# Short products with activations standing, and an accumulation by transfer into the residual tile, in a fused expert and state-space kernel on one Trainium2 core

## The reference

```python
x = x + 0.5 * ffn(layernorm(x), w_router, w_gating, w_gate, w_up, w_down)
x = x + attn(layernorm(x), W_in, conv_w, ..., W_out)      # a Mamba block
x = x + 0.5 * ffn(layernorm(x), w_router, ...)            # the same weights again

def ffn(x, ...):                       # E = 8 experts, F = 512; dense, every expert for every token
    cw = softmax(x @ w_router) * softmax(x @ w_gating / 0.1)
    cw = cw / (sum(cw) + 1e-9)         # 8 weights per token
    h[e] = silu(x @ w_gate[e]) * (x @ w_up[e])
    return sum_e (h[e] @ w_down[e]) * cw[:, e]

def attn(x, ...):                      # d_inner 256, 16 states, conv of 4, dt_rank 64
    xs, z = split(x @ W_in)            # 2 x 256
    xc = silu(causal_conv(xs) + conv_b)
    dt, B, C = from xc @ W_x           # dt = softplus(... @ W_dt + b_dt)
    h_t = exp(dt_t * A) * h_{t-1} + dt_t * xc_t * B_t     # per feature and state
    y = sum_n h[:, n] * C[n] + xc * D_param
    return (y * silu(z)) @ W_out
```

## Time and profile before

| | |
|---|---|
| time, median of 3 runs | 1301.04 us (1297.74 to 1301.64) |
| the profiled execution's own time | 1303.95 us |
| its span in the profile | 1302.2 us |
| PE busy | 1259.6 us, 97% |
| DVE busy | 1121.7 us, 86% |
| ACT busy | 925.3 us, 71% |
| POOL busy | 366.8 us, 28% |
| moved by DMA | 208.55 MB, mean 160 GB/s |

### The profile page before, as it was taken

The page is one execution under the profiler, slowest core; times in us unless marked ns, Lnnn a source line. Parts: engine busy times, 40 slices in busy tenths (PEclk is TensorE's granted clock), DMA queues, the critical chain, the costliest instruction groups (busy, mean ns, idle before and its releaser), DMA issues.

```text
span 1302.2 us, 15232 instructions
## 1 busy us (share of the span) xinstructions
PE 1259.6 (97%) x4608; PEld 841.3 (65%) x4608; DVE 1121.7 (86%) x1468; ACT 925.3 (71%) x1757; POOL 366.8 (28%) x438
## 2 busy tenths in 40 slices
PE   5999799999999999999999999999999999999998
PEld 4666566666666666666666666666666665666665
DVE  3554599999999999999989999999999998998343
ACT  6545688878797878887948878698866887653421
POOL 0100134324232322433323332342323323332000
PEclk9999899999999999999999999999999999999899
DMA  6521488789788988987888978987888786895221
GB/s 204 134 54 33 100 177 197 160 176 196 161 181 184 181 173 188 208 177 169 183 180 188 194 171 178 181 191 170 188 175 186 174 186 149 186 197 119 50 64 41
DMA packets 125809, 208.55 MB, mean 160 GB/s; under 512 B 15008, under 2 KB 27808, under 8 KB 125728
## 3 DMA queue, kind: packets, MB, share of 16 engines
q0 software_dynamic: 52128, 94.92, 40.8%
q1 hardware_dynamic: 73600, 112.68, 32.8%
HBM read 109.77 MB, written 2.88 MB: 87 GB/s over the span
## 4 chain that ended last, share of the span: by engine, by line
PE 65%; DMA 12%; ACT 9%; DVE 8%; issue 5%; POOL 2%; SPq 0%; DVEq 0%; ACTq 0%; POOLq 0%
PE PS L734 23%; PE PS L679 13%; PE PS L681 13%; PE PS L680 13%; DMA Y<-HS 7%; DMA ACC<-YE 3%; DVE HS L943 2%; DVE HB L851 2%; DVE HS L951 2%; ACT DA L1090 1%; ACT HB L1024 1%; DMA BCB<-BCD 1%; ACT L1024 1%; PE PS L755 1%; ACT L1090 1%
## 5 line engine op out<-in xcount | busy, mean ns | idle before, releaser
L734 PE MATMUL PS<-HB,WD 128*128 128x512 f32 x1024 | 525.3, 594 | 0.0
L1024 ACT ACTIVATE HB<-PS 128x512 f32<-128x512 f32 x512 | 293.1, 596 | 279.8 <-PE PS L681 277.4
L851 DVE TENSOR_TENSOR HB<-PS,HB 128x512 f32<-128x512 f32 x512 | 347.2, 679 | 113.9 <-PE PS L681 71.7
L679 PE MATMUL PS<-XH,WG 128*128 128x512 f32 x512 | 386.6, 755 | 6.1 <-DVE XH L906 2.0
L1139 POOL DMA_DIRECT2D Y<-HS x252 | 219.7, 949 | 511.0 <-DVE HS L951 319.5
L734 PEld LDWEIGHTS PS<-HB,WD 128*128 128x128 f32 x1024 | 191.8, 189 | 44.3 <-issue 3.4
L679 PE MATMUL PS<-XH,WU 128*128 128x512 f32 x512 | 209.5, 409 | 10.1 <-DVE HB L851 9.8
L1127 POOL DMA_DIRECT2D ACC<-YE x110 | 104.1, 947 | 369.3 <-DVE YE L841 339.4
L681 PE MATMUL PS<-XH,WG 128*128 128x512 f32 x512 | 203.2, 397 | 0.0
L681 PE MATMUL PS<-XH,WU 128*128 128x512 f32 x512 | 202.0, 395 | 0.0
L680 PE MATMUL PS<-XH,WU 128*128 128x512 f32 x512 | 201.0, 393 | 0.0
(11 more groups left out here) (104 smaller groups left out, 1127.3 us busy)
## 6 DMA issues: line engine op xcount, KB each, us to landing
BCB<-BCD SPq DMA_DIRECT2D x128, 512.0 KB, 5.6
Y<-HS POOLq DMA_DIRECT2D x252, 256.0 KB, 6.7
CWB<-CWD SPq DMA_DIRECT2D x128, 256.0 KB, 4.3
ACC<-YE POOLq DMA_DIRECT2D x110, 256.0 KB, 5.3
XT<-in_L_attn_x_dram SPq DMA_DIRECT2D x8, 256.0 KB, 5.9
WD<-in_L_ffn_w_down_dram SPq DMA_DIRECT2D x8, 256.0 KB, 6.1
out_dram<-XT SPq DMA_DIRECT2D x8, 256.0 KB, 3.1
HS<-in_L_ffn_w_gate_dram SPq DMA_DIRECT2D x6, 256.0 KB, 5.0
```

What stands on the lines that cost most here:

```text
L679: pe.matmul(o, w[0], m[0], start=first, stop=False)
L734: pe.matmul(expert(g), WD[:, e, c, :], HB[:, i % NH, :], start=c == 0, stop=c == FC - 1).then_inc(S["m_dn"], 1)
L851: v.tensor_tensor(H, up(i), H, ALU.mult).then_inc(S["v_h"], 1)
L1024: a.activation(HB[:, i % NH, :], gate(i), ACT.Silu).then_inc(S["a_sil"], 1)
```

## The change

- `down` has HB standing and WD moving: for each block of 128 tokens, one f32 product of 128 columns, so four in place of one of 512. The expert's bank then has tokens on partitions and output features along the row, like XT.
- The weights of a position stay per token row, in CW (two buffers). `p_ct`, `cwt`, CWD, its stores, CWB and `cw_load` go. `acc` multiplies the bank by CW[:, :, e] broadcast along the features, always into YE.
- The transfer adds YE straight into XT. Expert 0 is added in this way too. In the first and the last position the last expert is added on DVE by four scalar_tensor_tensor of 128x128 that multiply, add and write XT. ACC, `acc_t` and `acc_add` go; x1 is ready when the last add has landed, and ACT and SP wait for that.
- `s_out` has Y standing and WO moving: four blocks of tokens times two halves, eight f32 products of 128 columns. The copy to XN and `s_tr` go; `s_add` reads the bank of `s_out`.
- In `timetable()` the costs follow (`down` 0.9 for 0.86, `s_out` 1.78 for 1.75, the last step of a position 5.5 for 5.0, at the ends 0.9 for 1.25), and LEAD is 2.0 for 2.4.

```diff
-LEAD = 2.4
+LEAD = 2.0
...
     def weigh(g):
         if g % E < E - 1 or g // E not in ENDS:
-            at = step("acc", g, after=clock["pe"] + SIGNAL["pe"], v=.61, p=.9) + (5.0 if g % E == E - 1 else 0.0)
-        else:
-            at = step("acc", g, after=clock["pe"] + SIGNAL["pe"], v=1.25)
-        weights["used"] = g + 1
-        weight_loads()
-        return at
+            return step("acc", g, after=clock["pe"] + SIGNAL["pe"], v=.61, p=.9) + (5.5 if g % E == E - 1 else 0.0)
+        return step("acc", g, after=clock["pe"] + SIGNAL["pe"], v=.9)
 
     def tail(p):
         kind, t = ORDER[p]
         at = weigh(p * E + E - 1)
-        acc_done.add(p)
-        yield from until(at + 1.0)
-        bk = yield from take()
-        at = step("acc_t", p, bk, pe=.6)
-        yield from until_v(at)
-        at = step("acc_add", p, bk[0], after=at, v=.61)
-        give(bk[0], "v_x1", p + 1, at)
         if kind == 0:
             x1[t] = at
+        else:
+            yield from until(at)
+            step("out", t)
...
         yield from until(at)
-        yield from rows_of_x()
         bk = yield from take()
-        at = step("s_out", t, bk, xn["by"], after=at, pe=1.75, a=.52)
-        give(bk[0], "a_wo", t + 1, at)
+        at = step("s_out", t, bk, after=at, pe=1.78)
         put.add(t)
-        yield from until(at)
-        bk = yield from take()
-        at = step("s_tr", t, bk, pe=.6)
-        xn.update(by=("m_to", t + 1), lock=False)
...
                     wt.wait_ge(S["v_h"], i + 1)
-                    pe.matmul(expert(g), WD[:, e, c, :], HB[:, i % NH, :], start=c == 0, stop=c == FC - 1).then_inc(S["m_dn"], 1)
+                    for j in range(SUB):
+                        z = pe.matmul(expert(g)[:, j, :], HB[:, i % NH, j * P:(j + 1) * P], WD[:, e, c, :],
+                                      start=c == 0 and j == 0, stop=c == FC - 1 and j == SUB - 1)
+                    z.then_inc(S["m_dn"], 1)
...
-                    for j in range(2):
-                        z = pe.matmul(bank(b), WO[:, j, :], Y[:, t % 2, j, :], start=j == 0, stop=j == 1)
+                    for j in range(SUB):
+                        for c in range(2):
+                            z = pe.matmul(bank(b)[:, j * P:(j + 1) * P], Y[:, t % 2, c, j * P:(j + 1) * P], WO[:, c, :],
+                                          start=c == 0, stop=c == 1)
...
                     wt.wait_ge(S["m_dn"], FC * (g + 1))
-                    wt.wait_ge(S[f"c_cwb{g % CR}"], 16 * (g // CR + 1))
-                    if e == 0:
-                        if p:
-                            wt.wait_ge(S["m_tz"], p)
-                        y = ACC[:, :]
+                    wt.wait_ge(S["v_cw"], p + 1)
+                    if e == E - 1 and p in ENDS:
+                        wt.wait_ge(S["c_acc"], 16 * added(p, E - 1))
+                        for j in range(SUB):
+                            X = XT[:, ORDER[p][1] % XR, j, :]
+                            z = v.scalar_tensor_tensor(out=X, in0=expert(g)[:, j, :], scalar=CW[:, p % 2, j, e:e + 1], in1=X,
+                                                       op0=ALU.mult, op1=ALU.add)
+                        z.then_inc(S["v_ye"], 1)
                     else:
-                        n = p * (E - 1) + e - 1
+                        n = added(p, e)
                         if n >= 2:
-                            wait_summed(wt, n - 2)
-                        y = YE[:, n % 2, :]
-                    v.tensor_tensor(y, expert(g), CWB[:, g % CR, :], ALU.mult).then_inc(S["v_ye"], 1)
-                    if e == E - 1 and p in ENDS:
-                        wt.wait_ge(S["v_ye"], g + 1)
-                        wt.wait_ge(S["c_acc"], 16 * added(p, E - 2))
-                        v.tensor_tensor(ACC[:, :], ACC[:, :], y, ALU.add).then_inc(S["v_acc"], 1)
+                            wt.wait_ge(S["c_acc"], 16 * (n - 1))
+                        v.tensor_tensor(YE[:, n % 2, :, :], expert(g), CW[:, p % 2, :, e].unsqueeze(2).broadcast_to([P, SUB, P]),
+                                        ALU.mult).then_inc(S["v_ye"], 1)
...
-                        gp.dma_start(ACC[:, :], YE[:, n % 2, :], accum_op=ALU.add).then_inc(S["c_acc"], 16)
+                    gp.dma_start(XT[:, ORDER[p][1] % XR, :, :], YE[:, n % 2, :, :], accum_op=ALU.add).then_inc(S["c_acc"], 16)
```

More of the change, by code:

```diff
@@ L29 @@
 NB = 4 - NG
-CR = 3
 HR = 4
@@ L403, in timetable @@
         if i >= LAG:
-            step("down", i - LAG, after=h_at[i - LAG], pe=.86)
+            step("down", i - LAG, after=h_at[i - LAG], pe=.9)
             nd += 1
@@ L435, in timetable @@
     for i in range(nd, total):
-        step("down", i, pe=.86)
+        step("down", i, pe=.9)
     run(tail(NPOS - 1))
@@ L480, in macaron_program @@
         XH = sb("XH", [P, 2, 2, T], F32R)
-        CWB = sb("CWB", [P, CR, T])
-        YE = sb("YE", [P, 2, T])
-        ACC = sb("ACC", [P, T])
+        YE = sb("YE", [P, 2, SUB, P])
         HB = sb("HB", [P, NH, T])
@@ L515, in macaron_program @@
         S = {}
[L516 to L519, removed]
+        for n in ("c_small c_con c_acc c_y0 c_y1 c_bcd o_x init w_hi w_lo dv "
+                  "m_g m_u m_dn m_tr m_lg m_win m_wx m_wt m_wo "
+                  "a_sil a_sum a_mean a_sq a_xn a_car a_xf a_xh a_exp a_neg a_rmh a_win a_tap a_yc a_dbl a_abs a_relu a_sexp a_soft a_yd a_da "
+                  "v_h v_sub v_norm v_cw v_ye v_mset v_rm v_halo v_cv v_bc v_db v_sc v_hc v_yz v_x2 v_dt v_dx v_y v_xl "
                   "p_ve p_rs p_nm").split():
             S[n] = ctx.enter_context(nc.semaphore(n))
-        for b in range(CR):
-            S[f"c_cwb{b}"] = ctx.enter_context(nc.semaphore(f"c_cwb{b}"))
         for b in range(BR):
@@ L551, in expert @@
         def expert(g):
-            return PS[:, NG + 2 + g % 2, :]
+            return PS[:, NG + 2 + g % 2, :].rearrange("p (j d) -> p j d", j=SUB)
         def added(p, n):
-            return p * (E - 1) - (p > 0) + n
+            return p * E - (p > 0) + n
         def wait_position(eng, p):
             if p in ENDS:
-                eng.wait_ge(S["v_acc"], 1 + (p > 0))
+                eng.wait_ge(S["v_ye"], (p + 1) * E)
             else:
[L564 to L572, removed]
+                eng.wait_ge(S["c_acc"], 16 * added(p, E))
         def carried(m):
@@ L663, in _ @@
                     sy.dma_start(XT[:, t % XR, :, :], xf[t]).then_inc(S[f"c_x{t}"], 16)
-                elif s[0] == "acc_add" and ORDER[s[1]][0] == 1:
-                    t = ORDER[s[1]][1]
-                    wt.wait_ge(S["v_x1"], s[1] + 1)
+                elif s[0] == "out":
+                    t = s[1]
+                    wait_position(wt, POSITION[1, t])
                     if nout:
@@ L764, in _ @@
                 elif k == "s_out":
-                    _, t, (b, at), by = s
+                    _, t, (b, at) = s
                     wait_count(wt, at)
                     wt.wait_ge(S["v_yz"], t + 1)
-                    for j in range(2):
-                        z = pe.matmul(bank(b), WO[:, j, :], Y[:, t % 2, j, :], start=j == 0, stop=j == 1)
+                    for j in range(SUB):
+                        for c in range(2):
+                            z = pe.matmul(bank(b)[:, j * P:(j + 1) * P], Y[:, t % 2, c, j * P:(j + 1) * P], WO[:, c, :],
+                                          start=c == 0, stop=c == 1)
                     z.then_inc(S["m_wo"], 1)
[L771 to L777, removed]
         @block.vector
@@ L818, in _ @@
                     wt.wait_ge(S["dv"], dv)
[L819 to L823, removed]
-                    if p:
-                        wt.wait_ge(S["c_cwd"], 16 * SUB * p)
-                    v.transpose(cwt[:, :], pq[:, :, :].rearrange("p j e -> p (j e)")).then_inc(S["v_cw"], 1)
+                    v.scalar_tensor_tensor(out=CW[:, p % 2, :, :], in0=lg[:, :, 2, :], scalar=0.5,
+                                               in1=sm[:, :].unsqueeze(2).broadcast_to([P, SUB, E]), op0=ALU.mult, op1=ALU.mult).then_inc(S["v_cw"], 1)
                 elif k == "acc":
@@ L851, in _ @@
                     v.tensor_tensor(H, up(i), H, ALU.mult).then_inc(S["v_h"], 1)
-                elif k == "acc_add":
-                    _, p, b = s
-                    X = XT[:, ORDER[p][1] % XR, :, :].rearrange("p j d -> p (j d)")
-                    wt.wait_ge(S["m_tz"], p + 1)
-                    v.tensor_tensor(X, X, bank(b), ALU.add).then_inc(S["v_x1"], 1)
                 elif k == "w_split":
```

60 lines of the change are left out of this document (11 added, 49 removed).

## The result

The changed kernel takes 1281.13 us (median of 4 runs, 1280.6 to 1281.49) against 1301.34 us before: ratio 0.9835, 95% interval 0.982 to 0.985, or 20.2 us less. The forecast was 1291, 10 us less. The direction was right and the size was not: the gain is twice the one that was summed.

The account below looks back on a forecast made before the run. PE, 97% busy, was taken as nearly full with DVE close behind; +22 +0.6 -3.5 -7.0 -24.8 +5 -1.7 = -9.4 us against the profiled execution, carried to the runs' median as 1291 us, range 1277 to 1313.

Parts of the forecast that it names:

- The products down: Each `down` on PE: eight load-paced pairs of 0.112 us, 0.90 us against 0.857, +22 us over 512 slots.
- The first rival: Eight pairs of each `down`: weight loads don't hide fully, 1316 at 0.118 a pair, 1353 at full 0.015; chance 0.18.
- the ratio that the prediction worked out from the Trainium skill: Each `down`: four short products cost 2.5 times one long one, 2.12 us, kernel up by about 645 us.
- SP's queue: CWB loads and CWD stores hold places ahead of BCB loads; removing them saves PE 9.1 us, and 1.3 at 185 to 191.
- The state stage's output: `s_out` as 16 pairs +0.6 us; `s_tr` gone -3.5 us of PE, plus its waits of 5.4 us.
- The end: Last multiply, add, transposes, add of 2.94 us become four scalar_tensor_tensor of 1.2 in all: -1.7 us.
- the named waits: PE waits in SP's queue (9.1, 1.3), `acc_t` (3.7), `s_tr` (5.4) and before the last position (5.3): -24.8 us.
- I give back +5 us, a fifth: Part of the removed PE waits returns, through ScalarE's wait for x1 and stalls of the new order: +5 us.
- the third rival: DVE was the true bound: with 27 us less on it PE's small waits shrink, nothing is given back, 1279; chance 0.15.

Follow-up runs that it names:

- the four other orders: Changed kernel with LEAD 1.8, 2.2 or 2.4, or at LEAD 2.0 with the planner's `down` cost 0.86: 1291.61, 1292.64, 1293.29, 1290.58 us.
- The second attempt: Changed kernel, planner starting a tile's stream `before` 1.5 us after its x1's planned landing: 1284.9 us at LEAD 2.4, 1280.18 at LEAD 2.2.

## Why the size was wrong, step by step

**The products down: right.** 0.90 us was forecast and 0.90 measured, a slot of 2.28 forecast and measured, a spacing of 0.112. The first rival needed 0.115 a pair. A load of 0.112 runs wholly under a product that was estimated at 0.108. The idea that each change of weights costs 0.015 us fell. So did the ratio that the prediction worked out from the Trainium skill, "TensorE: Matmul & The Clock Gate", Back-to-back issue gap: four short products cost 1.05 times one long one in f32 here, and not 2.5 times. The logits, with 16 columns moving, priced it because the load sets the pace in both.

**But not all of it shows.** The sum charged +22 us in full. Added PE work is absorbed by a third in the old kernel. In the changed kernel I can't separate that share from the others.

**SP's queue: right**, 8.2 us alone for 9.1 forecast. **The state stage's output: right in size**, 7.0 for 8.3, across two orders. **The end: right**, -1.8 for -1.7.

**The step that failed** is the net of the waits. The prediction booked -24.8 us for the named waits, "I give back +5 us, a fifth", and left the small waits of PE as they were, so some 20 us net. By the count above PE's idle time after 100 us fell by 36 us. It divides like this.
- The named waits all left. In the kernel before the parts from 142 to 157.5, 198 to 204, 672 to 680, 942 to 952, 1074 to 1090 and 1210 to 1223 us hold 28.8 us of idle time, where 24.8 were booked. So these were booked 4 us short.
- Nothing came back, and the give-back of 5 us had the wrong sign. Beside the named waits the kernel before has 15.7 us of idle time after 100 us, of which 1.8 belong to the end, priced by itself; the changed kernel has 8.4 in all. So the other waits did not grow by 5 us, they shrank by some 5.5. This is the third rival's case, "nothing is given back", with its 1279 and its -8 for small waits. Its mechanism, DVE's relief, is shown in part by the 9.8 us of the run with more DVE work. Its name, DVE as the true bound, doesn't fit: DVE is 98.1 of 100 us busy beside a PE that doesn't wait.
- "The add into x1 that PE stood for is now waited for by ScalarE ... Only tile 1 needs its x1 at once; the other tiles' are older." The first sentence was right, the second wrong. The norms of tiles 5, 6 and 7 (at about 671, 829 and 988 us) waited in three of the four other orders, and those of 6 and 7 in the fourth; tile 1 waited long in one only. By the planner's list at LEAD 2.4 the norms of tiles 2 to 4 come 14 slots or more after the last multiply of their expert layer, those of tiles 5 to 7 at most one slot after. The age that the first tiles have was carried over to tiles where it doesn't hold. The change as made pays almost nothing for it, 0.8 us of ScalarE's time.

**Luck.** LEAD 2.0 was part of the change, but nothing in the prediction foresaw that with it the adds land before the norms ask for them. Tiles 6 and 7 have their norms two and three slots later than with LEAD 2.4 (slots 324 and 388 for 322 and 385, by the planner's list), and the adds have landed. Tile 5 is in slot 259, and it is in slot 259 with LEAD 2.2 and 1.8 too, where it waits 7.1 and 6.3 us. There the add landed 7.6 and 7.9 us after its issue, by the trace, close behind two adds of POOL into Y. In the changed kernel it landed after 3.3, with POOL idle ahead of it, and ScalarE was at exponentials and silus until 665.53 anyway:

```profile
660.96 0.86 POOL L1045 DMA_DIRECT2D XT<-YE  x1 [7.69 <-DVE YE L773]
```

```profile
661.08 1.75 POOL L1057 DMA_DIRECT2D Y<-HS  x2 [3.90 <-DVE HS L875]
663.41 0.86 POOL L1045 DMA_DIRECT2D XT<-YE  x1 [0.58 <-DVE YE L773]
```

(The first is the changed kernel, the second LEAD 2.2.) That 1291 falls among the 1290.6 to 1293.3 of the four other orders is luck as well: they pay for waits that the sum held to be free, and have gains that it left out.

**What stays open.** LEAD 1.8 to 2.4 and the planner's cost were each changed alone; why the order at 2.0 and 0.9 puts two of those norms later was not followed through the planner. The second attempt moved other steps with the norms too, so the 8.4 and 12.5 us are the wait together with what else moved. How LEAD 2.0 does in the old kernel was not tried: its queues would lock each other there. The two smaller causes, absorption and DVE's relief, overlap, and their shares in the waits that shrank aren't told apart.

## What to carry to other kernels

Price short products by the pace of their weight loads, read from any group in the trace with that stationary form, and not by record lengths or by a ratio from other types. When a removed step had a wait in it, find who waits for the same event now, and check it at every tile, not at the first; then put the waiting step later in its queue. In a kernel whose order is planned ahead, an edit that touches the plan carries a throw with it, here of some 10 us: time the same instructions in two or three other orders before crediting the instructions.

## What the runs showed of the hardware that I had not expected

The hiding of loads is complete down to a near tie: eight loads of 0.112 us under eight f32 products, estimated at 0.108 us each by a quarter of the long one's spacing, give 0.90 us, with under 0.01 us at the seam. The windows of the changed kernel give a PE clock of 1.00 from 100 to 1200 us, where the kernel before has 0.99. Its windows of 100 us have 0.97 from 100 to 200 and 0.98 from 600 to 700 and from 1000 to 1100, and these hold the waits of 6.74, 2.26 and 2.58 us; the half-clock stretches stood behind such waits and left with them. Four scalar_tensor_tensor of 128x128 with a PSUM operand take 1.13 us, 0.345 in the mean of one record, where the line between the 128x32 and 128x512 rows gave 0.30. And the transfers that add into their target land faster in the changed kernel than before, in a median 4.5 us against 5.3 by the page of the profile; the kernel moves 29 MB less. By the trace of the changed kernel the landing goes with what POOL issued just before: the 46 adds into XT that were issued less than 3 us after an add into Y landed in a median 6.6 us, another 79 in 4.1.
